# A third decay place in SBUF for the unit ahead of each pair of gate silus

## What is computed

```python
def ffn(x):                              # 0.5 * ffn(layernorm(x)) is added
    h = silu(x @ w_gate) * (x @ w_up)    # 512 -> 2048
    return keep_2_of_4(h) @ w_down

def mamba(x):                            # E = 1024, N = 16
    xn = rmsnorm(x) * norm_w
    skip, u = xn @ W_skip.T, silu(conv4(xn @ W_in.T))
    delta = softplus(u @ Wd1.T @ Wd2.T + bd2)
    B, C, A = u @ WB.T, u @ WC.T, -exp(A_log)
    # over the positions l, for each e and n:
    #   h = exp(delta * A) * h + delta * u * B_n ;  y = sum_n h * C_n
    return ((y + u * W_D) * silu(skip)) @ W_out.T
```

## Time and profile before

| | |
|---|---|
| runs | 3604.5, 3607.23, 3607.34 us; median 3607.23 |
| span of the profiled execution, first to last instruction | 3600.7 us (the profile gives no other time for it) |
| PE busy | 3360.2 us, 93% |
| DVE busy | 3027.7 us, 84% |
| POOL busy | 2594.9 us, 72% |
| ACT busy | 2061.7 us, 57% |
| DMA | 193 GB/s over the span |
| mean granted TensorE clock | 0.979 |

### The profile page before, as it was taken

The page is one execution under the profiler, slowest core; times in us unless marked ns, Lnnn a source line. Parts: engine busy times, 40 slices in busy tenths (PEclk is TensorE's granted clock), DMA queues, the critical chain, the costliest instruction groups (busy, mean ns, idle before and its releaser), DMA issues. The chain is left out here.

```text
span 3600.7 us, 39012 instructions
## 1 busy us (share of the span) xinstructions
PE 3360.2 (93%) x11958; PEld 2122.7 (59%) x12020; DVE 3027.7 (84%) x3597; ACT 2061.7 (57%) x2805; POOL 2594.9 (72%) x1625
## 2 busy tenths in 40 slices
PE   8999999999999999999999999988989889988899
PEld 6775566556655665566555565555545555555467
DVE  5546998788999889988898899988998988999934
ACT  5546657567565765566565675565555566454422
POOL 1316876667877779768787678868888878979913
PEclk9999999999999999999999999999999989999999
DMA  9656566657756676566665675647646556645433
GB/s 356 219 188 192 176 207 222 205 176 221 215 175 210 202 227 200 171 203 208 187 205 176 202 230 169 221 138 215 222 124 210 172 178 220 187 149 184 139 120 114
DMA packets 243470, 696.45 MB, mean 193 GB/s; under 512 B 23536, under 2 KB 23792, under 8 KB 233584
## 3 DMA queue, kind: packets, MB, share of 16 engines
q1 hardware_dynamic: 173632, 559.72, 45.1%
q10 hardware_dynamic: 69632, 134.23, 15.6%
HBM read 619.94 MB, written 76.55 MB: 193 GB/s over the span
## 5 line engine op out<-in xcount | busy, mean ns | idle before, releaser
L1381 POOL TENSOR_TENSOR scan_in<-du,scan_rows 128x512 f32<-128x512 f32 x1024 | 1312.8, 1294 | 700.9 <-DVE decay L1255 612.1
L1255 DVE TENSOR_TENSOR_SCAN decay<-decay,scan_in 128x512 f32<-128x512 f32 x1024 | 1252.4, 1223 | 157.0 <-ACT decay L865 150.9
L865 ACT ACTIVATE decay<-delta,small 128x512 f32<-128x512 f32 x1024 | 699.4, 689 | 935.4 <-DVE scan_out L1265 928.7
L1394 POOL TENSOR_TENSOR y<-y,scan_out 128x1024 f32<-128x1024 f32 x512 | 1227.0, 2397 | 0.6 <-DVE scan_out L1265 0.6
L637 PE MATMUL main<-zhi,wunit 128*128 128x512 f32 x2048 | 909.9, 444 | 62.1 <-DVE cmp L1195 38.3
L729 PE MATMUL side<-h,wdown 128*128 128x512 f32 x1760 | 801.8, 599 | 24.2 <-ACT sq L988 12.6
L639 PE MATMUL main<-zhi,wunit 128*128 128x512 f32 x2048 | 817.7, 399 | 0.0
L638 PE MATMUL main<-zlo,wunit 128*128 128x512 f32 x2048 | 816.7, 399 | 0.0
L1265 DVE TENSOR_TENSOR scan_out<-decay,scan_rows 128x512 f32<-128x512 f32 x1024 | 702.9, 686 | 27.6 <-POOL y L1394 2.2
L729 PEld LDWEIGHTS side<-h,wdown 128*128 128x128 f32 x1760 | 334.5, 191 | 392.7 <-issue 350.2
L637 PEld LDWEIGHTS main<-zhi,wunit 128*128 128x128 f32 x2048 | 390.2, 191 | 233.6 <-issue 89.5
(11 more groups left out here) (117 smaller groups left out, 3192.8 us busy)
## 6 DMA issues: line engine op xcount, KB each, us to landing
wunit<-hl_dram SPq DMA_DIRECT2D x480, 512.0 KB, 4.3
scan_rows<-bc_dram ACTq DMA_DIRECT2D x256, 512.0 KB, 5.7
wdown<-down_w_dram SPq DMA_DIRECT2D x256, 256.0 KB, 3.2
wmam<-mam_dram SPq DMA_DIRECT2D x128, 512.0 KB, 4.1
hl_dram<-wunit SPq DMA_DIRECT2D x32, 512.0 KB, 4.6
skip_dram<-skb SPq DMA_DIRECT2D x64, 256.0 KB, 4.2
delta<-skip_dram SPq DMA_DIRECT2D x16, 1024.0 KB, 6.7
wmam<-wout_dram SPq DMA_DIRECT2D x32, 512.0 KB, 4.3
```

The costliest lines, as they stand in the source:

```text
L865: nc.scalar.activation(decay[u % BANKS][:], delta[:, e, :], ACT.Exp, scale=aneg[:, e * N + n:e * N + n + 1]).then_inc(sem["decay_ready"], 1)
L1255: nc.vector.tensor_tensor_scan(decay[u % BANKS][:], decay[u % BANKS][:], db[u % INPUTS][:], 0.0, ALU.mult, ALU.add).then_inc(sem["state_re ...
L1381: nc.gpsimd.tensor_tensor(db[u % INPUTS][:], du[:, e, :], rows[m % ROWS][:, 0, :], ALU.mult).then_inc(sem["input_ready"], 1)
L1394: nc.gpsimd.tensor_tensor(y[:, e:e + 2, :], y[:, e:e + 2, :], scan_out[:, k:k + 2, :], ALU.add).then_inc(sem["sum_ready"], 1)
```

## The change

A third place for decays, `spare`, is added in SBUF, where `skb` was; it holds only chosen units. `place_decays` chooses them: at every tick whose ACT work begins with gate silus and that has at least two units, the second unit of the tick is special (95 of them; never the first of all). Its exponential is issued at the end of the tick before, ahead of the silus; scan and product of that unit work in place in `spare`. The other units go on alternating between the two banks, and each waits for the last unit that used its place (`freed_by`), which for the two units behind a special one is one unit further back than before. `load_rows` waits explicitly for the products that read the old rows.

Skip silus use `dts` instead of `skb` (for sequence 0 the first tile of `zm`). For this ACT waits, before the first skip of a sequence, for the last `dl` job of the sequence before (or for the split of x), before the copy of dt for all skip stores; DVE waits before the first norm after M of sequence 0 for that sequence's skip stores. The late half of the `dl` jobs moves from ticks `STARTS[b] + 8`, `+ 9` to `+ 7`, `+ 8`. The planner's cost of a `dl` job is zero, so `units_at` stays as it was.

```diff
--- before.py
+++ after.py
@@ -148,7 +148,7 @@
             self.jobs_at[origin + chain["bc"] + 1].append(("fold", b))
             for e in range(HE):
                 self.jobs_at[origin + chain["dl"] + (e // 2 if chain is SLOW else 0)].append(("dl", b, e))
-                self.jobs_at[STARTS[b] + 8 + e // 2].append(("dl", b, HE + e))
+                self.jobs_at[STARTS[b] + 7 + e // 2].append(("dl", b, HE + e))
             late = STARTS[b] + 8
             self.first_at[origin + chain["first"]] = (b, 0)
             self.first_at[late + 2] = (b, 1)
@@ -226,7 +226,25 @@
                     self.units_at[t] = range(done, upto)
                     done = upto
         assert done == B * UNITS
+        self.place_decays()
         self.tick_of_unit = {u: tick for tick, units in enumerate(self.units_at) for u in units}
+
+    def place_decays(self):
+
+        self.extra_at = {}
+        for tick in range(1, self.ticks):
+            n, units = self.product_at[tick - 1], self.units_at[tick]
+            if n is not None and n % 4 == 1 and len(units) > 1 and units.start:
+                self.extra_at[tick - 1] = units.start + 1
+        extra, last, turn = set(self.extra_at.values()), {}, 0
+        self.decay_of, self.freed_by = [], []
+        for u in range(B * UNITS):
+            k = BANKS if u in extra else turn
+            if u not in extra:
+                turn = (turn + 1) % BANKS
+            self.decay_of.append(k)
+            self.freed_by.append(last.get(k))
+            last[k] = u
 
     def place_weights(self):
 
@@ -322,10 +340,11 @@
         db = [scan_in[:, k, :] for k in range(INPUTS)]
         pr = [scan_out[:, k, :] for k in range(RING)]
         cv = [sb(f"cv{k}", [P, L]) for k in range(2)]
-        skb = sb("skb", [P, L])
         sq = sb("sq", [P, KD, L])
         parts, rt, rs = sq[:, 0, :], sq[:, 1, :], sq[:, 2, :]
         dts = sb("dts", [P, L])
+        spare = sb("spare", [P, L])
+        skip_buffer = lambda b: dts[:] if b else zm[:, 0, :]
         raw_x = [delta[:, k, :].rearrange("p (k m) -> p k m", k=KD) for k in range(KE)]
         raw = [y[:, k, :].rearrange("p (k m) -> p k m", k=KD) for k in range(RAWS)]
 
@@ -339,7 +358,8 @@
 
         main = [pb(f"main{k}") for k in range(MAINS)]
         side = [pb(f"side{k}") for k in range(SIDES)]
-        decay = [pb(f"decay{k}") for k in range(BANKS)]
+        decays = [pb(f"decay{k}") for k in range(BANKS)] + [spare]
+        decay = lambda u: decays[plan.decay_of[u]]
 
         sem = {name: ctx.enter_context(nc.semaphore(name)) for name in (
             "product_ready", "side_ready", "gate_read", "up_read", "part_ready",
@@ -499,7 +519,7 @@
                 for key in plan.jobs_at[tick - 2] if tick > 1 else []:
                     if key[0] == "skip":
                         wait_read(sp, key)
-                        sp.dma_start(skip_dram[key[1]][:, key[2], :], skb[:]).then_inc(sem["skip_stored"], 16)
+                        sp.dma_start(skip_dram[key[1]][:, key[2], :], skip_buffer(key[1])).then_inc(sem["skip_stored"], 16)
                     if key[0] == "fold":
                         wait_read(sp, key)
                         sp.dma_start(bc_dram[key[1] % 2].rearrange("k n l -> (k n) l"), bcs).then_inc(sem["bc_stored"], 16)
@@ -860,9 +880,9 @@
                 e += HE * half
                 if v == 0:
                     wait_delta(act, b, half)
-                if u >= BANKS:
-                    act.wait_ge(sem["weighted_ready"], u - BANKS + 1)
-                nc.scalar.activation(decay[u % BANKS][:], delta[:, e, :], ACT.Exp, scale=aneg[:, e * N + n:e * N + n + 1]).then_inc(sem["decay_ready"], 1)
+                if plan.freed_by[u] is not None:
+                    act.wait_ge(sem["weighted_ready"], plan.freed_by[u] + 1)
+                nc.scalar.activation(decay(u)[:], delta[:, e, :], ACT.Exp, scale=aneg[:, e * N + n:e * N + n + 1]).then_inc(sem["decay_ready"], 1)
                 if u % HE == BANKS - 1:
                     load_rows(u // HE + 2)
 
@@ -876,6 +896,8 @@
 
                 if m >= B * GROUPS:
                     return
+                if m >= ROWS:
+                    act.wait_ge(sem["weighted_ready"], HE * (m - ROWS + 1))
                 b, n = m // GROUPS, m % N
                 if m % GROUPS < 2:
                     act.wait_ge(sem["bc_stored"], 16 * (b + 1))
@@ -1011,10 +1033,17 @@
                 wait_job(act, key)
                 if KE * b + e:
                     act.wait_ge(sem["skip_stored"], 16 * (KE * b + e))
-                nc.scalar.activation(skb[:], bank_of(key)[:], ACT.Silu).then_inc(read_of(key), 1)
+                if e == 0:
+                    if b:
+                        wait_job(act, ("dl", b - 1, KE - 1))
+                    else:
+                        act.wait_ge(sem["x_low_ready"], KD)
+                nc.scalar.activation(skip_buffer(b), bank_of(key)[:], ACT.Silu).then_inc(read_of(key), 1)
 
             def copy_dt(key):
                 wait_job(act, key)
+                if key[1]:
+                    act.wait_ge(sem["skip_stored"], 16 * KE * (key[1] + 1))
                 nc.scalar.activation(dts[:], bank_of(key)[:], ACT.Copy).then_inc(read_of(key), 1)
 
             def copy_parts(key):
@@ -1120,6 +1149,8 @@
                 if tick in plan.first_at:
                     first_terms(*plan.first_at[tick])
                 upto(share(units, 3, 4).stop)
+                if tick in plan.extra_at:
+                    upto(plan.extra_at[tick])
 
 
         @block.vector
@@ -1130,6 +1161,8 @@
                 wait_job(dve, key)
                 if kind == "M" and b:
                     dve.wait_ge(sem["m_loaded"], 16 * b)
+                if key[1] == plan.norm_of["M", 0] + 1:
+                    dve.wait_ge(sem["skip_stored"], 16 * KE)
                 if key[1] in plan.alone:
                     for k in range(KD):
                         nc.vector.tensor_tensor(zm[:, k, :], x[:, k, :], bank_of(key)[:],
@@ -1252,7 +1285,7 @@
             def scan(u):
                 dve.wait_ge(sem["decay_ready"], u + 1)
                 dve.wait_ge(sem["input_ready"], u + 1)
-                nc.vector.tensor_tensor_scan(decay[u % BANKS][:], decay[u % BANKS][:], db[u % INPUTS][:], 0.0, ALU.mult,
+                nc.vector.tensor_tensor_scan(decay(u)[:], decay(u)[:], db[u % INPUTS][:], 0.0, ALU.mult,
                                              ALU.add).then_inc(sem["state_ready"], 1)
 
             def times_c(u):
@@ -1262,7 +1295,7 @@
                 dve.wait_ge(sem["state_ready"], u + 1)
                 if u >= RING:
                     dve.wait_ge(sem["sum_ready"], (u - RING) // 2 + 1)
-                nc.vector.tensor_tensor(pr[u % RING][:], decay[u % BANKS][:], rows[m % ROWS][:, 1, :], ALU.mult).then_inc(sem["weighted_ready"], 1)
+                nc.vector.tensor_tensor(pr[u % RING][:], decay(u)[:], rows[m % ROWS][:, 1, :], ALU.mult).then_inc(sem["weighted_ready"], 1)
 
             def begin(units):
 
```

## The result

The changed kernel runs at 3657.4 us (median of 4 runs, 3656.2 to 3659.7), the kernel before beside it at 3606.9 us. The ratio is 1.0144, with a 95% interval of 1.0131 to 1.0158: 50.5 us slower. A second comparison on another chip gave 1.0145. Forecast were 3636 us, a range of 3586 to 3680, and slower with a chance of 0.60.

A forecast was written before the change was run, and what follows sets the result against it. PE was taken to bound 400 to 2000 us, DVE 2000 to 3400. DVE's 104.5 - 62.2 = +42 us passed as 18 late and 8 early; with POOL's 3, 3607.2 + 29 = 3636 us, range 3586 to 3680.

The forecast's parts named there:

- the lock's price: Special scans and products on DVE wait for POOL over SBUF: 1.1 us a unit, 104.5 us for 95 units.
- the share that passes to the end: Of DVE's net loss, all of the 40 late units' 18 us and a third of the early 25 us lengthen the run.
- DVE is the bound of the second stretch, PE of the first: PE bounds 400 to 2000 us (idle 55 us, DVE 185); DVE bounds 2000 to 3400 us (idle 109, PE 147).
- The gain, 62.2 us: DVE's 55 waits for the decay of a tick's second unit, behind gate silus, vanish: 62.2 us back.
- I put no wait there: At the third unit, ACT's 4.4 us to its decay is covered by DVE's 3.8 us plus the unit in hand.
- The first meeting: The special scan on DVE waits for a running POOL instruction: 0.58 to 0.75 us a unit, taken as 0.65.
- The second meeting: The product right behind the special scan waits for POOL in about a quarter of cases: 0.45 us a unit.
- The break-even of 0.65 us a unit: Lock price for each special unit at which DVE's loss equals the 62.2 us gained.
- The rule of the port pair: A DVE instruction with two SBUF inputs and a GpSimd instruction reading SBUF exclude each other for a whole instruction.
- POOL's ring: POOL, shut out for 181 us, may leave DVE meeting a full ring: bound 0 to 20 us, taken 3.
- the rows' load: Its wait for the last product holds ACT's silus at 26 places, 0.5 us each at most: 0 to 13, taken 0.
- The late half of delta: Its matmuls and softplus come one tick earlier, moving ACT's hole: -5 to +5 us, taken 0.

The follow-up runs named there:

- the moves alone: Changed kernel with no special units: no SBUF place used, no early exponential; dts, new waits and earlier late half of delta kept; 3594.6 us.
- the lead and one PSUM operand: Changed kernel, but special scans and products read their second operand from the previous unit's PSUM bank (numbers of these units wrong); 3573.4 us.

## Why the prediction was right or wrong

The direction, the range and the mechanism held: two SBUF operands beside POOL cost more than the lead gives back. Of the terms of the sum, the lock's price was sized too low and the share that passes to the end was wrong.

*DVE is the bound of the second stretch, PE of the first.* Of little use as it stood. It made me let a third of the first stretch's loss pass. The runs give 0.78 there and 0.84 later. DVE's slack summed over a stretch (100 us idle outside its decay waits) did not take up the loss. That it lies in other ticks than the special units is my reading; what the traces show is that PE also lost time by the lower granted clock. The sign named for this step failed too: PE's waits for DVE should have grown after 2000 us and hardly before, and summed over the lists of waits they grew from 40.3 to 52.2 us before 2000 and from 116.5 to 131.9 after.

*The gain, 62.2 us.* Right where it was looked for: those 55 waits are gone, and the list of waits fell by 71.5. But it is not what the lead is worth. Without the port DVE still waits 102.4 us, so the lead removes 45. "I put no wait there", for the third unit, was wrong: its waits grow from 12.3 us in 8 places with the moves alone to 24.4 us in 22 with the lead and one PSUM operand. And of these 45 only 21 us reach the end.

*The lock's price, 1.1 us a unit.* The mechanism was right, and the runs show it by the single operand: 1.46 us with two SBUF operands, nothing with one. The first meeting was taken at 0.65 us and measured 0.83; with the exponential in the old order it was 0.57. It was priced as the rest of one POOL instruction, and for 86 of the 95 scans that was right. Ahead of the other 9 further POOL instructions ran, which cost 19.2 us more, 0.20 us for each of the 95; without that the first meeting is 0.62. The second meeting was taken at 0.45 and measured 0.63, because 48 of 95 products waited, 1.25 us in the mean, and not a quarter of them. Together the port took 138.8 us where 104.5 were forecast. The same price stood for both stretches, and the late one was 1.79. The break-even of 0.65 us a unit was passed by far.

*The rule of the port pair in the Trainium skill* ("SBUF — State Buffer", section "SBUF: two separate sides") holds for the scan too: 1210 ns at the least and 5526 at the most with two SBUF inputs, 1205 to 1217 with one. The fixed term of the Trainium skill that speaks for SBUF ("VectorE: DVE Perf Modes", section on the TRN2 errata) did not show: the shortest scan with both operands in SBUF took 1210 ns and the shortest with one in PSUM 1212, the products 691 and 671, where an estimate by it was 65 ns each.

*POOL's ring, 3 us, and the rows' load, 0.* POOL's own instructions grew by 80 us in all (62 ns x 1024 and 33 ns x 512), but DVE waited for the ring as little as before. The rows' load was bounded at 0.5 us a place, and ACT waited up to 7.2 us in one (31.7 us in 15); even so it held up nothing that can be told.

*The late half of delta, 0.* Wrong by 10.5 to 12 us, in the other direction than the change as a whole. I had bounded it by ACT's hole (-5 to +5) and had not asked which side banks PE would find free one tick earlier.

The steps by which the runs go from the kernel before to the changed one are -10.5 for the moves, +83.5 for the place and -20.7 for the lead; they add up by construction, to 52.3 us, where the direct comparison gave 50.5. How the forecast of +29 missed is told by the two kernels with the special units of one stretch. DVE's net loss was forecast at 25 us early and 18 late and was 31.8 and 44.0. With the forecast's own shares, a third and all, that alone adds 29 us (10.6 + 44.0 - 26), nearly all of it late, where the port's price was furthest off. The true shares add 7 more: 14 early, less 7 late. The moves take 10.5 off, and POOL's 3 never came. That gives 51, so the undersized price was the larger miss, and the unforeseen gain of the moves hid part of both by luck.

## What to carry to other kernels

Before a tile moves from PSUM to SBUF, look at every VectorE instruction that reads it: if its other operand is in SBUF and GpSimd works on SBUF beside it, the instruction can have to wait for GpSimd, as it did here when it started while one of GpSimd's ran, and the list of waits does not show it, only the mean and the maximum of its group. Take the price of such a meeting from the moment at which the instruction will run after the change, because work that comes earlier can meet the other engine in another state: the first meeting cost 0.57 us in the old order and 0.83 in the new one. Do not write a loss of one engine off against another engine's being the bound, unless a run shows it: 0.78 of the early loss came through. Test each side effect of a change alone: the one-tick move that was carried along was worth 12 us, and the part meant to help cost 63.

## What the runs showed of the hardware

A VectorE instruction that waits for the port can be passed over by more than one GpSimd instruction. In the earlier trace rows it got in between two of them; in the changed kernel some did not. The longest of the special scans, on DVE's and then POOL's timeline of the changed kernel:

```profile
3173.18 0.68 DVE L1298 TENSOR_TENSOR scan_out<-decay,scan_rows 128x512 f32<-128x512 f32 x1
...
3173.77 5.53 DVE L1288 TENSOR_TENSOR_SCAN spare<-spare,scan_in 128x512 f32<-128x512 f32 x1
...
3179.34 0.69 DVE L1298 TENSOR_TENSOR scan_out<-spare,scan_rows 128x512 f32<-128x512 f32 x1
...
3171.06 2.38 POOL L1427 TENSOR_TENSOR y<-y,scan_out 128x1024 f32<-128x1024 f32 x1
...
3173.40 2.49 POOL L1414 TENSOR_TENSOR scan_in<-du,scan_rows 128x512 f32<-128x512 f32 x2
...
3175.85 2.37 POOL L1427 TENSOR_TENSOR y<-y,scan_out 128x1024 f32<-128x1024 f32 x1
```

The scan is ready at 3173.8 us. POOL then finishes one instruction, runs another of 1.26 us and one of 2.37, back to back, until 3178.2, and the scan ends 1.1 us after that, at 3179.3: 5.53 us in all. I had priced a first meeting at no more than the rest of one instruction. 5 of the 95 special scans take more than 3.7 us, which is more than a whole one of POOL's longer form (2.4 us) and the scan itself. On the timelines 9 of the 95, 7 of them after 2000 us, had one or two whole POOL instructions run after they were ready and ahead of them, besides the one that was running; in the other 76 that met a running instruction DVE came next. What decides which of the two is served next is left open by these runs.
